# All 32 quads of the recurrent stage written out on four engines, in a graph-RNN and mixture-of-experts kernel

## The chip, the cores and the metric

The kernel runs on one core of one Trainium2 chip. Five engines with instruction streams of their own work in it: TensorE (PE in the rows; its weight loads are PEld), VectorE (DVE), ScalarE (ACT), GpSimd (POOL) and SyncE (SP). They agree by semaphores. The metric is device time in microseconds (us). Before the change the median of three runs is 710.54 us.

## The reference

x is 128 batches of 128 tokens of 128 features, adj is 128 matrices of 128 x 128.

```python
beta = _layernorm(x) @ e_weight / max(sum(adj, 2), EPS)
agg = einsum('blu,blm->bmu', beta, adj)
h_t = tanh(agg[:, t] @ Wx + h_{t-1} @ Wh + b)         # 128 steps, one after the other
x1 = x + h
z = _layernorm(x1)
topk_vals, topk_idx = top_k(z @ gate_w + gate_b, 2)   # 16 experts, 2 for each token
moe = sum_k softmax(topk_vals)_k * expert_{topk_idx_k}(z)
out = x1 + _layernorm(z + moe) * gamma + beta_ffn
```

## The kernel before

The work has three stages. In the first (0 to about 77 us) the batches are normalised and aggregated. In the second, the recurrent stage (about 77 to 285 us), the 128 steps of the recurrence run, and each finished token is normalised, gated, counted and sent as a row to the memory region of its expert. In the third the experts run over the sorted rows. Everything in the front of the kernel belongs to one block; the third stage is a second block, and the engines meet between the two (line 858).

The recurrent stage goes by quads: four steps of the recurrence make a quad, so there are 32. Slots in SBUF are reused every 8 quads (SLOTS).

- PE, `steps(q, u)`: four times a matmul with Wh (L455) onto the aggregate that `fresh` (L446) put in PSUM; between them the transposes of the last quad's states (`turn_h`, L408), the counting matmuls of quad q - 3 (`count`, L437 to L440, which wait for DVE's `hot`), the gate's logits of q - 2 (`logits`, L425) and the transposes of x1 (`turn_x`, L416).
- ACT, `steps(q, u)`: four tanh (L554), and between them copies, exponentials, and for each quad one part of centring W2.
- DVE, `turn(q, u)`: 23 small parts for quads q - 1, q - 2 and q - 3, in an order written out by hand. It opens with `tile_a` (L624: x1 = x + h, which waits for PE's transposes, for the load of x2r, and from the ninth quad for the sends out of its slot), has `gate_3` (L710) and `gate_5` (L730, `hot`) in it, and `place_3` (L766) puts the destination rows of quad q - 3.
- POOL, `turn(q, u)`: `send(q - 3)`, four indirect DMAs (L222) that scatter the rows of one quad each 128 rows at a time; it waits for `tokens` of ACT, `soft_3` and `place_3` of DVE.
- SP loads x2r four quads ahead (L256).

The order of instructions on an engine is the order in the source. `quads(eng, body, 8)` writes quads 0 to 7 out and then runs a loop of three turns whose body holds eight quads. In the loop the quad number is a register, so each wait whose value depends on it needs register arithmetic ahead of it. PE's stage has quads 0 to 7 written out, a loop of two turns of eight (quads 8 to 23), and quads 24 to 31 written out. After its loop DVE has three written-out turns (32 to 34), and POOL three sends. `hold` waits on `s_const` first and then on the semaphore, with a constant or a register alike.

Once DVE's last `place_3` is done, POOL has the last sends to do, DVE makes the tables of the third stage (L820 to L856, with PE's L491), and SP and ACT issue the padding (L211). Then the block ends.

Of the kernel before, what the change touches and what calls it, by code (L numbers as in the profile page):

```python
# [15 lines left out]
NQ = P // QUAD  # L16
SLOTS = 8
# [16 lines left out]

def build(nc, x, adj, eW, Wx, Wh, b, gate_w, gate_b, w1, b1, w2, b2, gamma, beta, out):
    NE, _, F = w1.shape
    NBLK = P + NE
    NQUAD = NBLK // QUAD
# [8 lines left out]
    with ExitStack() as ctx:  # L47
# [177 lines left out]
        def beyond(q, n):  # L225

            return not (isinstance(q, int) and q < n)

        def quads(eng, body, n=UN):

            for u in range(n):
                body(u, u)
            with eng.Fori(1, NQ // n) as J:
                for u in range(n):
                    body(n * J + u, u)
# [54 lines left out]
        def _(pool):  # L290
# [37 lines left out]
            def send(q, u):  # L328

                hold(pool, s_tok, q + 1)  # L330
                pool.wait_ge(s_w1, q + 1)
                hold(pool, s_d, q + 1)
                for j in range(QUAD):
                    scatter(dram_a.ap(), st[:, u, j, C_POS1:C_POS1 + 1].bitcast(I32), st[:, u, j, :],
                            ROWS).then_inc(s_sct[u], 16)
# [39 lines left out]
            def turn(q, u):  # L375
                if beyond(q, 3):
                    send(q - 3, (u - 3) % SLOTS)
            quads(pool, turn, SLOTS)
            for k in range(3):
                send(NQ - 3 + k, SLOTS - 3 + k)  # L380

# [2 lines left out]
        def _(pe):  # L384
# [19 lines left out]
            def turn_h(q, u):  # L404
                if beyond(q, 1):
                    pe.wait_ge(s_x1, q)
                for j in range(QUAD):
                    i = nc.tensor.transpose(ps_ht[:, j * P:(j + 1) * P], HT[:, u % 2, j * P:(j + 1) * P], ident[:, :])  # L408
                i.then_inc(s_ht, 1)

            def turn_x(q, u):
                pe.wait_ge(s_x1, q + 1)
                if beyond(q, 1):
                    pe.wait_ge(s_xe, q)
                for j in range(QUAD):
                    i = nc.tensor.transpose(ps_xt[:, j * P:(j + 1) * P], st[:, u % SLOTS, j, 0:P],  # L416
                                            ident[:, :])
                i.then_inc(s_xt, 1)

            def logits(q, u):  # L420
                pe.wait_ge(s_xe, q + 1)
                if beyond(q, 1):
                    pe.wait_ge(s_l1, q)
                for j in range(QUAD):
                    i = mm(ps_lg[:, j * NE:(j + 1) * NE], x1T[:, u % 2, j * P:(j + 1) * P], gwc[:, :],  # L425
                           start=True, stop=True)
                i.then_inc(s_lg, 1)

            def count(q, u):

                pe.wait_ge(s_hot, q + 1)
                if beyond(q, 2):
                    pe.wait_ge(s_pos, q - 1)

                o, w = ps_agg[u % 2], 2 * NE
                m = hot[:, u % 2, w:]
                mm(o[:, 0:5 * w], ones[:, :], hot[:, u % 2, :], start=True, stop=False, skip_group_check=True)  # L437
                mm(o[:, 0:4 * w], tri[:, :], m, start=False, stop=False, skip_group_check=True)
                for k in range(3, 0, -1):
                    i = mm(o[:, (5 - k) * w:5 * w], ones[:, :], m[:, 0:k * w], start=False, stop=k == 1,  # L440
                           skip_group_check=True)
                i.then_inc(s_cnt, 1)

            def fresh(q, u):

                return mm(ps_rnn[u % 2][:, :], Ec[:, :], AX[:, bass.ds(QUAD * q, QUAD), :], start=True, stop=True,  # L446
                          skip_group_check=True)

            def steps(q, u):

                for k in range(QUAD):
                    if k or beyond(q, 1):
                        pe.wait_ge(s_th, QUAD * q + k)
                        h = (u if k else u - 1) % 2
                        mm(ps_rnn[u % 2][:, k * P:(k + 1) * P], Wh_sb[:, :],  # L455
                           HT[:, h, ((k - 1) % QUAD) * P:((k - 1) % QUAD + 1) * P], start=False, stop=True,
                           skip_group_check=True).then_inc(s_rn, 1)
                    if k == 0 and not (isinstance(q, int) and q == NQ - 1):
                        fresh(q + 1, u + 1)
                    if k == 1 and beyond(q, 1):  # L460
                        turn_h(q - 1, u - 1)
                    if k == 2 and beyond(q, 3):
                        count(q - 3, u - 3)
                    if k == 2 and beyond(q, 2):
                        logits(q - 2, u - 2)
                    if k == 3 and beyond(q, 1):
                        turn_x(q - 1, u - 1)
# [1 line left out]
            quads(pe, agg, SLOTS)  # L469
            pe.wait_ge(s_ae, NQ)  # L470
            fresh(0, 0).then_inc(s_rn, 1)
            for u in range(SLOTS):
                steps(u, u)
            with pe.Fori(1, NQ // SLOTS - 1) as J:
                for u in range(SLOTS):
                    steps(SLOTS * J + u, u)
            for u in range(SLOTS):
                steps(NQ - SLOTS + u, u)
            pe.wait_ge(s_th, P)
            turn_h(NQ - 1, UN - 1)  # L480
            count(NQ - 3, UN - 3)
# [14 lines left out]
        def _(act):  # L496
# [18 lines left out]
            def agg_out(q, u):  # L515
                act.wait_ge(s_m1, q + 1)
                nc.scalar.copy(AX[:, :, bass.ds(QUAD * q, QUAD)],
                               ps_agg[u % 2][:, :].rearrange("p (b t) -> p t b", b=QUAD)).then_inc(s_ae, 1)
# [12 lines left out]
            def exps(q, u):  # L531
                act.wait_ge(s_dd, q + 1)
                if beyond(q, 2):
                    act.wait_ge(s_w1, q - 1)
                a(ex[:, u % 2, :], dd[:, u % 2, :], ACT.Exp).then_inc(s_ex, 1)
# [46 lines left out]

            quads(act, first, SLOTS)
            agg_out(NQ - 1, UN - 1)
            quads(act, steps, SLOTS)
            exps(NQ - 3, UN - 3)
            sums(NQ - 3, UN - 3)
            x1T_out(NQ - 2, UN - 2)
# [10 lines left out]
        def _(dve):  # L599
# [201 lines left out]
            def turn(q, u):  # L801


                order = ((tile_a, 1), (soft_2, 3), (tile_b, 1), (soft_3, 3), (place_1, 3), (tile_b2, 1), (place_2, 3),
                         (tile_b3, 1), (gate_1, 2), (root_0, 1), (place_3, 3), (sq_0, 1), (gate_2, 2),
                         (ag_0, 1), (gate_3, 2), (in_0, 1), (gate_4, 2), (ou_0, 1), (sq_1, 1), (gate_5, 2), (ag_1, 1),
                         (in_1, 1), (ou_1, 1))
                for part, lag in order:
                    if beyond(q, lag) and not (isinstance(q, int) and q - lag >= NQ):
                        part(q - lag, (u - lag) % SLOTS)  # L810
            quads(dve, turn, SLOTS)
            for q in range(NQ, NQ + 3):
                turn(q, q % SLOTS)

            dve.wait_ge(s_d, NQ)
# [398 lines left out]
```

## Time and profile before

| | |
|---|---|
| median of 3 runs | 710.54 us (709.33 to 710.82) |
| the profiled execution | 710.99 us |
| its span in the trace | 709.0 us |
| mean granted TensorE clock | 0.89 of 2.4 GHz |
| busy: PE, DVE, ACT, POOL | 77%, 76%, 58%, 66% of the span |

The profiled execution is 2.0 us longer than its span and 0.45 us longer than the median. Times in the rows are us from the start of the span. A bracket at a row's end is the idle time of the engine ahead of the instruction, and what ended it ("issue": nothing that the profile shows).

### The profile page before, as it was taken

Reading aid. Unit: us, or ns where it says so; the run is one execution under the profiler, and the core shown is the slowest. Engines: PE = TensorE matmul, PEld = TensorE weight load, DVE = VectorE, ACT = ScalarE, POOL = GpSimd, SP = SyncE. Lnnn points to the kernel's source line nnn. Section 1 sums busy time; section 2 is a strip of 40 time slices with the busy share of each in tenths; the row PEclk is TensorE's granted clock in tenths of the full one; section 3 lists DMA queues with packets and bytes.
Section 4 is the critical chain, followed back from the end, with each engine's and each line's share of the span. In section 5 each row is a group of like instructions: output and inputs, shape, how many; then the busy total and the mean of one; then the engine's idle time right before and its main releaser. Section 6 shows DMA issues by size and latency. Waiting matters only on the chain.

```text
span 709.0 us, 18043 instructions
## 1 busy us (share of the span) xinstructions
PE 544.5 (77%) x4140; PEld 486.8 (69%) x4140; DVE 539.0 (76%) x2791; ACT 407.8 (58%) x1345; POOL 466.6 (66%) x526
## 2 busy tenths in 40 slices
PE   1766789887888873399999999800799999999920
PEld 1655566665666652399999999800789999999920
DVE  5988599897997997288888888700299999999950
ACT  2889655454554540266666666500588888888810
POOL 3666647675765767067777777776067777777774
PEclk9989999897987985599999999955799999999975
DMA  8999649432332313379885665430997676664110
GB/s 216 282 281 282 158 147 278 143 104 75 96 94 84 97 49 114 80 210 334 258 251 192 202 190 185 150 149 28 294 328 231 191 215 202 208 203 142 49 49 7
DMA packets 115098, 121.40 MB, mean 171 GB/s; under 512 B 19017, under 2 KB 99613, under 8 KB 115008
## 3 DMA queue, kind: packets, MB, share of 16 engines
q1 hardware_dynamic: 95936, 76.79, 38.7%
q0 software_dynamic: 17920, 43.03, 16.7%
q8 instruction: 34, 0.56, 0.4%
q10 hardware_dynamic: 1152, 0.56, 0.3%
q14 instruction: 56, 0.46, 0.2%
HBM read 68.67 MB, written 55.90 MB: 176 GB/s over the span
## 4 chain that ended last, share of the span: by engine, by line
PE 38%; POOL 7%; ACT 7%; issue 4%; DMA 1%; DVE 1%; SPq 1%; POOLq 0%; ACTq 0%; DVEq 0%
PE bank L987 19%; PE bank L1003 15%; ACT hs L1055 4%; POOL rows_by_second L222 4%; POOL out_dram L222 3%; PE bank L976 3%; ACT xT L1036 2%; PE bank L1000 2%; DMA R<-rows_by_second 0%; DMA rows_by_second<-R 0%; DMA R<-rows_by_first 0%; ACT wr L1044 0%; SPq L912 0%; ACT L1064 0%; SPq L914 0%
## 5 line engine op out<-in xcount | busy, mean ns | idle before, releaser
L222 POOL DMA_INDIRECT rows_by_second<-R x144 | 146.2, 1015 | 62.2 <-issue 36.6
L222 POOL DMA_INDIRECT out_dram<-R x144 | 143.2, 994 | 66.7 <-issue 38.7
L1055 ACT ACTIVATE hs<-bank,wr 128x128 f32<-128x128 f32 x432 | 127.5, 368 | 86.7 <-PE bank L987 82.7
L1003 PE MATMUL bank<-W,hs 128*128 x1152 | 176.1, 289 | 0.0
L222 POOL DMA_INDIRECT rows_by_first<-st x128 | 125.3, 979 | 76.6 <-ACT st L546 40.2
L987 PE MATMUL bank<-xT,wr 128*128 128x128 f32 x1152 | 159.1, 282 | 7.2 <-ACT xT L1036 6.7
L1003 PEld LDWEIGHTS bank<-W,hs 128*128 128x128 f32 x1152 | 151.7, 192 | 3.5
L987 PEld LDWEIGHTS bank<-xT,wr 128*128 128x128 f32 x1152 | 143.1, 196 | 14.6 <-ACT xT L1036 13.4
L1124 DVE SCALAR_TENSOR_TENSOR R<-bank,R 128x128 f32<-128x128 f32 x288 | 87.6, 346 | 66.6 <-PE bank L1003 63.2
L1044 ACT COPY wr<-W1b 128x258 f32 x288 | 105.0, 427 | 14.7 <-PEq L858 14.7
L554 ACT ACTIVATE HT<-bank,bcol 128x128 f32<-128x128 f32 x128 | 46.7, 365 | 69.6 <-PE bank L455 65.7
L976 PE MATMUL bank<-ident,R 128*128 128x128 f32 x288 | 45.0, 281 | 54.0 <-DMA R<-rows_by_second 40.9
L976 PEld LDWEIGHTS bank<-ident,R 128*128 128x128 f32 x288 | 35.1, 146 | 54.7 <-DMA R<-rows_by_second 41.1
L1036 ACT COPY xT<-bank 128x512 f32<-128x512 f32 x72 | 42.9, 595 | 47.7 <-PE bank L976 47.7
L455 PEld LDWEIGHTS bank<-HT,Wh_sb 128*128 128x128 f32 x254 | 45.8, 212 | 35.0 <-ACT HT L554 29.7
L455 PE MATMUL bank<-HT,Wh_sb 128*128 128x128 f32 x254 | 62.3, 331 | 3.3 <-ACT HT L554 2.3
L1000 PE MATMUL bank<-b2s,sel 128*128 128x128 bf16 x288 | 63.2, 219 | 0.4 <-ACT hs L1055 0.3
L400 PE MATMUL bank<-aq,xs 128*128 128x128 f32 x256 | 42.2, 319 | 24.9 <-ACT xs L511 24.8
L400 PEld LDWEIGHTS bank<-aq,xs 128*128 128x128 f32 x256 | 36.4, 221 | 30.7 <-ACT xs L511 19.2
L1113 DVE TENSOR_SCALAR hs<-bank,wr 128x128 f32<-128x128 f32 x144 | 43.8, 346 | 10.3 <-PE bank L987 10.3
L1102 DVE TENSOR_SCALAR R<-R 128x128 f32<-128x128 f32 x144 | 42.2, 366 | 11.7 <-DMA R<-rows_by_first 11.7
L511 ACT ACTIVATE xs<-xq,scq 128x128 f32<-128x128 f32 x128 | 40.8, 391 | 10.0 <-POOL scq L325 9.1
(137 smaller groups left out, 875.4 us busy)
## 6 DMA issues: line engine op xcount, KB each, us to landing
R<-rows_by_second SPq DMA_DIRECT2D x144, 196.0 KB
R<-rows_by_first SPq DMA_DIRECT2D x144, 68.0 KB
xq<-in_x_dram SPq DMA_DIRECT2D x32, 256.0 KB, 4.0
aq<-in_adj_dram SPq DMA_DIRECT2D x32, 256.0 KB, 5.0
x2r<-in_x_dram SPq DMA_DIRECT2D x32, 256.0 KB, 2.9
rows_by_second<-filler SPq DMA_DIRECT2D x1, 3136.0 KB, 13.7
rows_by_second<-filler SPq DMA_DIRECT2D x16, 196.0 KB
rows_by_second<-R POOLq DMA_INDIRECT x144
```

What stands on the lines that cost most here:

```text
L222: return nc.gpsimd.indirect_dma_start(dst, bass.IndirectOffsetOnAxis(ap=idx, axis=0), src, None, bounds_check=limit[n], oob_is_err=False)
L400: i = mm(ps_agg[u % 2][:, j * P:(j + 1) * P], xs[:, u % 2, j * P:(j + 1) * P], aq[:, u, j * P:(j + 1) * P], start=True, stop=True)
L455: mm(ps_rnn[u % 2][:, k * P:(k + 1) * P], Wh_sb[:, :], HT[:, h, ((k - 1) % QUAD) * P:((k - 1) % QUAD + 1) * P], start=False, stop=True, sk ...
L554: a(HT[:, u % 2, k * P:(k + 1) * P], ps_rnn[u % 2][:, k * P:(k + 1) * P], ACT.Tanh, bias=bcol[:, :]).then_inc(s_th, 1)
L976: i = nc.tensor.transpose(ps_z[:, j * P:(j + 1) * P], R[:, u, j, C_Z:C_Y], ident[:, :])
L987: i = mm(ps_h[c][h][:, (j % 2) * P:(j % 2 + 1) * P], wr[:, u % 2, j, c * P:(c + 1) * P], xT[:, u % 2, j * P:(j + 1) * P], start=True, stop ...
L1000: mm(o, sel[:, bass.ds(e[k], 1), :].rearrange("p o m -> p (o m)"), b2s[:, :], start=True, stop=False, skip_group_check=True)
L1003: i = mm(o, hs[:, h, c, k * P:(k + 1) * P], W2[:, bass.ds(e[k], 1), c, :].rearrange("p o f -> p (o f)"), start=False, stop=c == 1, skip_gr ...
L1036: nc.scalar.copy(xT[:, u % 2, :], ps_z[:, :]).then_inc(e_xe, 1)
L1044: i = nc.scalar.copy(wr[:, u % 2, j, :], W1b[:, bass.ds(e, 1), :].rearrange("p o f -> p (o f)"))
L1055: i = a(hs[:, h, c, k * P:(k + 1) * P], ps_h[c][h][:, k * P:(k + 1) * P], ACT.Relu, bias=wr[:, u % 2, 2 * h + k, F + c:F + c + 1])
L1124: i = v.scalar_tensor_tensor(out=y, in0=ps_o[h][:, k * P:(k + 1) * P], scalar=R[:, u, j, w:w + 1], in1=y if r else R[:, u, j, C_Z:C_Y], op ...
```

## The change

On POOL, PE, ACT and DVE the loops of the recurrent stage are replaced by Python loops over all quads, so that every quad has its own instructions and every wait a constant. The work, its order on each engine and all buffers stay. SP's loop stays, and so do the loops of the first stage (`quads(pe, agg)`, `quads(act, first)`, `quads(dve, stats)`, `quads(pool, scale)`) and those of the third.

```diff
@@ gpsimd
-            quads(pool, turn, SLOTS)
+            for q in range(NQ):
+                turn(q, q % SLOTS)
@@ tensor
             fresh(0, 0).then_inc(s_rn, 1)
-            for u in range(SLOTS):
-                steps(u, u)
-            with pe.Fori(1, NQ // SLOTS - 1) as J:
-                for u in range(SLOTS):
-                    steps(SLOTS * J + u, u)
-            for u in range(SLOTS):
-                steps(NQ - SLOTS + u, u)
+            for q in range(NQ):
+                steps(q, q % SLOTS)
@@ scalar
-            quads(act, steps, SLOTS)
+            for q in range(NQ):
+                steps(q, q % SLOTS)
@@ vector
-            quads(dve, turn, SLOTS)
-            for q in range(NQ, NQ + 3):
+            for q in range(NQ + 3):
                 turn(q, q % SLOTS)
```

## Rows read from the trace of the kernel before

**Rows 1.** Waits by engine and line, longest in total first, 76.7 to 288.7 us

```profile
engine line waited for: us in total, times, longest us
ACT HT L554 <- PE bank L455: 65.7, 84, 3.7
...
PE bank L437 <- DVE hot L730: 24.3, 22, 2.9
...
DVE st L624 <- issue: 7.8, 8, 3.3
```

**Rows 2.** Busy time of each engine per stretch: written-out turns 4 to 6, then loop turns

```profile
core 0: us, PE busy (x) PEld busy (x) DVE busy (x) ACT busy (x) POOL busy (x), PEclk, DMA share, GB/s
98.70:104.27 5.57, 4.58 (x36) 3.44 (x33) 5.23 (x42) 3.08 (x12) 4.21 (x5) 1.00 0.73 235
104.27:109.56 5.29, 5.27 (x27) 3.99 (x27) 5.09 (x42) 2.55 (x10) 3.94 (x5) 0.69 1.06 354
109.56:114.84 5.28, 4.97 (x39) 3.77 (x37) 5.08 (x42) 3.42 (x13) 3.93 (x5) 0.98 1.04 337
...
150.76:156.42 5.66, 4.37 (x32) 3.23 (x32) 5.34 (x40) 2.88 (x11) 3.89 (x5) 1.00 0.31 97
156.42:162.04 5.62, 5.62 (x32) 4.28 (x31) 5.35 (x40) 2.59 (x11) 3.88 (x5) 0.70 0.34 99
162.04:171.26 9.22, 5.82 (x44) 4.48 (x41) 5.41 (x40) 4.23 (x16) 6.17 (x7) 1.00 0.26 76
```

**Rows 3.** Timeline of DVE: openings of turns 3, 9, 10 and 15; start, duration

```profile
93.47 0.69 DVE L624 TENSOR_TENSOR st<-bank,x2r 128x512 f32<-128x512 f32 x1
...
128.33 0.69 DVE L624 TENSOR_TENSOR st<-bank,x2r 128x512 f32<-128x512 f32 x1 [2.13 <-DMA x2r<-in_x_dram]
...
133.90 0.69 DVE L624 TENSOR_TENSOR st<-bank,x2r 128x512 f32<-128x512 f32 x1
...
162.04 0.69 DVE L624 TENSOR_TENSOR st<-bank,x2r 128x512 f32<-128x512 f32 x1
```

**Rows 4.** Timeline of DVE at the first jump back of its loop

```profile
167.79 0.17 DVE L680 SCALAR_TENSOR_TENSOR st<-root_a,root_y 128x4 f32<-128x4 f32 x1
171.26 0.69 DVE L624 TENSOR_TENSOR st<-bank,x2r 128x512 f32<-128x512 f32 x1 [3.31 <-issue]
```

**Rows 5.** Timeline of DVE: the second jump back, then turns 31 and 32

```profile
210.65 0.69 DVE L624 TENSOR_TENSOR st<-bank,x2r 128x512 f32<-128x512 f32 x1
...
219.80 0.69 DVE L624 TENSOR_TENSOR st<-bank,x2r 128x512 f32<-128x512 f32 x1 [3.23 <-issue]
...
261.88 0.27 DVE L766 TENSOR_REDUCE st<-picked 128x8 int32<-128x128 f32 x1
...
265.15 0.69 DVE L624 TENSOR_TENSOR st<-bank,x2r 128x512 f32<-128x512 f32 x1
```

**Rows 6.** DMA queues, 167 to 171.5 us: queue, kind, packets, MB, share

```profile
q14 instruction: 3, 0.02, 2.1%
```

**Rows 7.** DMA queues, 133.9 to 156.42 us, the same columns

```profile
q14 instruction: 3, 0.02, 0.3%
```

**Rows 8.** Timeline of all engines where PE's and ACT's loops jump back

```profile
163.78 0.30 PEld L455 LDWEIGHTS bank<-HT,Wh_sb 128*128 128x128 f32 x2 [0.26 <-ACT HT L554]
...
164.31 0.37 ACT L554 ACTIVATE HT<-bank,bcol 128x128 f32<-128x128 f32 x1 [0.29 <-PE bank L455]
```

**Rows 9.** Timeline of PE's transposes of the states, just ahead of turn 15

```profile
160.75 0.70 PE L408 MATMUL bank<-ident,HT 128*128 128x128 f32 x4
```

**Rows 10.** Timeline of DVE's place_3 in turn 9, and POOL's sends behind it

```profile
131.05 0.28 DVE L766 TENSOR_REDUCE st<-picked 128x8 int32<-128x128 f32 x1
...
132.14 0.97 POOL L222 DMA_INDIRECT rows_by_first<-st  x1 [2.88 <-ACT st L546]
133.42 0.97 POOL L222 DMA_INDIRECT rows_by_first<-st  x1 [0.30 <-issue]
```

**Rows 11.** Timeline of POOL: the last four quads, first three sends and last send

```profile
263.06 0.97 POOL L222 DMA_INDIRECT rows_by_first<-st  x1 [0.74 <-issue]
265.71 0.98 POOL L222 DMA_INDIRECT rows_by_first<-st  x1 [1.68 <-issue]
267.00 0.97 POOL L222 DMA_INDIRECT rows_by_first<-st  x1 [0.30 <-DVE st L742]
...
283.59 0.97 POOL L222 DMA_INDIRECT rows_by_first<-st  x1 [0.30 <-issue]
```

**Rows 12.** Timeline of DVE, ACT and SP at the end of the stage

```profile
282.69 0.30 DVE L856 TENSOR_SCALAR sti<-si 1x296 int32<-1x296 int32 x1
...
288.67 1.33 ACT L1044 COPY wr<-W1b 128x258 f32 x4 [14.68 <-PEq L858]
...
288.96 3.28 SPq L912 DMA_DIRECT2D R<-rows_by_first  x6
```

## The prediction

> **What bounds the kernel now.** I read the waits first, because the edit touches four engines and only the one that the others wait for can matter. In the recurrent stage ACT waits for PE (65.7 us, every tanh for its matmul), and PE waits for DVE's `hot` (24.3 us), which stands ahead of the counting matmuls in PE's order [rows 1]. DVE's own largest wait has no releaser: 7.8 us of "issue" ahead of `tile_a`, the first instruction of a turn [rows 1]. So the question is what DVE is doing. The busy time by stretch, each stretch one turn of DVE (from one L624 to the next), answers it: DVE is busy 5.08 to 5.41 us in every turn, whether the turn takes 5.28 or 9.22, while PE, in the shorter turns at a granted clock of 0.98 or more, has 4.4 to 5.0 [rows 2]. DVE is the bound; it sets the pace of `hot`, so of PE's count, so of the recurrence.
>
> Then I compare turns that are written out with turns in the loop, since both kinds are in this trace with the same work. Turns 3 to 6, written out, run from 93.47 [rows 3] to 114.84 [rows 2]: 21.37 / 4 = 5.34 us each. Turns 10 to 14, in the loop, run from 133.90 to 162.04 [rows 3]: 28.14 / 5 = 5.63 us each. Turn 15 of DVE ends with the jump back, and takes 9.22 us [rows 2]; all of its excess, 9.22 - 5.63 = 3.59 us, lies in one gap of 3.31 us (and the register work that belongs to every turn) between L680, the last instruction of the body, and L624, the first [rows 4]. The second jump makes a turn of 219.80 - 210.65 = 9.15 us, an excess of 3.52 us [rows 5].
>
> What is in that gap? The DMA queues show three instruction packets of queue 14 in the 4.5 us around the jump, where 22.5 us inside the loop have three as well [rows 6, 7]: code is fetched again when the jump is taken. The Trainium skill (Runtime: NRT & Kernel Launch, section Instruction fetch mechanics) says that a taken branch to code outside the two blocks held forces a fetch before execution goes on, while the next block of straight code is fetched ahead. The trace agrees with the first half by the 3.31 us gap.
>
> The end of the stage is not DVE's but POOL's. DVE finishes the tables at 282.69 + 0.30 = 282.99; POOL's last send starts at 283.59 and takes 0.97, so it ends at 284.56 [rows 11, 12]. The third stage opens at 288.67 (ACT) and 288.96 (SP's loads) [rows 12], some 4.1 us after POOL.
>
> **The change part by part.**
>
> DVE's jumps (removed): 3.59 + 3.52 = 7.11 us of DVE's path, nothing beside them.
>
> DVE's register work (removed in turns 8 to 31): a loop turn costs 5.63 - 5.34 = 0.29 us more than a written-out one. Its own spread bounds this: the written-out turns themselves are 5.57, 5.29 and 5.28 [rows 2]. With all new turns at 5.28 the difference is 0.35, with all at 5.57 it is 0.06. I take the mean over four turns, as it has both kinds in it.
>
> What is late next on DVE: `tile_a` of turn 9 waits 2.13 us for the load of x2r [rows 3]. SP's order is not touched, so that load lands when it did, and all that turns 1 to 8 save is lost there. I count from 128.33 on. Turn 32 opens at 265.15 [rows 5]: 23 turns in 136.82 us. Written out: 23 x 5.34 = 122.8. DVE gains 14.0 us, of which 7.1 are the jumps and 6.9 the registers.
>
> POOL: its sends of quad 6 start at 132.14, 0.81 us after `place_3` of turn 9 ends at 131.05 + 0.28 [rows 10]. `place_3` of turn 31 is at 261.88 [rows 5], 22 turns and 130.83 us later; written out these are 22 x 5.34 = 117.5, a gain of 13.35 us. POOL could become the bound instead: a send comes every 133.42 - 132.14 = 1.28 us, so a quad takes 5.11 us at least [rows 10]. That is under 5.34, so it keeps up, by 0.23 us a turn. From 263.06 POOL has 16 sends, and needs 284.56 - 263.06 = 21.50 us; at 1.277 each less the last pause of 0.30 they are 20.13. The other 1.37 us is one pause of 1.68 us in the last turn of its loop, ahead of 265.71, which no other send of the stage has and which nothing releases [rows 11]. It stands where the body of the loop runs for the last time. If it belongs to the loop it goes, if to the sends it stays: POOL gains 14.7 or 13.35. I take that it goes, since within the written-out sends nothing like it is seen, and keep the other for the range. DVE's last work, 14.0 us earlier at 269.0, stays ahead of POOL's end at 284.56 - 14.7 = 269.9, so POOL ends the stage still.
>
> PE and ACT: their jumps cost nothing now. Where PE's loop jumps back it waits 0.26 us for the tanh, as it does in other quads, and ACT at its own jump 0.29 us for PE [rows 8]. Their register work lies in the time in which PE waits for DVE. Both edits at nothing; what hides them is DVE's pace, and that cover gets thinner. PE at a mean granted clock of 0.70 is busy for all 5.62 us of a turn, and its transposes end at 160.75 + 0.70 = 161.45, 0.59 us before DVE needs them at 162.04 [rows 2, 3, 9]. A turn that is 0.29 shorter leaves 0.30. Against a loss stands the written-out turn of 104.27 to 109.56: at 0.69 it took 5.29 all the same [rows 2]. I put 0.5 us on it in all (an estimate), between 0 and 2.2 (one of the three loop turns shown is such a one; eight of 24 at 5.62 - 5.34 each).
>
> Fetching more code: DVE's code gets longer, but it executed each of these instructions before; in turns 3 to 6 it ran straight code at 5.34 with the fetches in it. Nothing.
>
> The waits for a slot's sends, which quads 8 and later have and quads 0 to 7 have not, come as constants. They are met eight quads before, so only the issue of the instruction that carries them could cost; turn 4, the slowest of the written-out ones, has 5.57 without them, so a cost of up to 0.23 us a turn can't be told from such scatter. I take 0, and leave the other end to rival A.
>
> The third stage starts earlier and is else the same, with its clock in the same low state at its start. So I move the end by POOL's gain.
>
> Sum, against the profiled execution: 710.99 - 14.7 + 0.5 = 696.8 us. That execution is 0.45 us above the median of the runs, so the median after should be 696.3 us.
>
> **The rivals.**
>
> A, only the jumps go. The 0.29 us of a loop turn is not register arithmetic but something that late quads carry in any form (the slots' waits, or how DVE's code falls), as the 5.57 turn, written out, hints. Then the gain is 7.1 us: 710.5 - 7.1 = 703.4. Against it: turns 12 and 13 took 5.66 and 5.62 beside 97 and 99 GB/s of DMA, and turns 5 and 6, written out, 5.29 and 5.28 beside 354 and 337 [rows 2].
>
> B, PE takes the bound in its slow stretches. At half clock (1.2 GHz granted, which is what a mean of 0.70 is made of together with 2.4) PE fills a turn of 5.62. If each such turn stays at 5.62 the price is 2.2 us, 1.7 more than in the sum, and with POOL's pause kept another 1.4: 696.3 + 1.7 + 1.4 = 699.4.
>
> C, slower. Straight code stalls DVE at each new block of code as the jump does. Rows 7 put an instruction packet on queue 14 every 7.5 us or less often; even if only every second one is DVE's, 136 us have 9. At 3.3 us each that is 30 us, less the 14 gained: 726. It decides from 14 / 9 = 1.6 us a block. Against it: the written-out turns 3 to 6, 21 us, took at most 5.57 each, so none has such a gap in it [rows 2]. The skill's rule of the same section (straight code is fetched ahead, a crossing is mostly hidden) would make this case nothing; only the rows bear on the chance.
>
> D, the change doesn't do what it says: the tool that builds the kernel could keep the loop or its register waits. The written-out quads 0 to 7 show that it doesn't.
>
> E, better: all turns at 5.28. Then DVE gains 136.82 - 121.4 = 15.4, POOL 130.83 - 116.2 + 1.37 = 16.0: 694.5.
>
> **How the numbers follow.** Forecast, 695.5 to 698.5: 0.58. B, with partial forms, 698.5 to 702: 0.17. A, 702 to 705: 0.10. E, below 695.5: 0.10. C: 0.03. D: 0.02. The likeliest time is 696.3. The range takes in E down to 693.8 and B up to 702.0, and leaves A, C and D out, 0.15, and a little below. Faster by over 0.2% (which is about what a measurement of this kernel can tell from no change): 0.95. Same: 0.02. Slower: 0.03.
>
> **What would show it.** In the profile after: no "issue" gap over 1 us ahead of L624; DVE's turns from 128.33 on at 5.3 to 5.4 us, turn 32 near 251.2; the wait for x2r in turn 9 still there and somewhat longer; PE and ACT with fewer register instructions and the same waits on DVE; POOL's last send ending near 270 without a pause of 1.7; the third stage as long as before. The prediction is wrong if turns stay at 5.6 (A), if `tile_a` begins to wait for L408 (B), or if gaps of some 3 us come at even distances on DVE (C).

## The result, and the profile after

| | before | after |
|---|---|---|
| median of 5 runs | 710.54 us | 697.5 us (696.34 to 698.12) |
| the profiled execution | 710.99 us | 697.93 us |
| its span | 709.0 us | 696.1 us |
| busy: PE, DVE, ACT, POOL | 77, 76, 58, 66% | 77, 77, 59, 67% |

The ratio is 0.982, with a 95% interval of 0.981 to 0.983: the kernel is 13.0 us faster. The forecast was 696.3, in a range of 693.8 to 702.0.

The waits, sorted as in [rows 1], come first again (columns: us in total, times, longest):

```profile
engine line waited for: us in total, times, longest us
ACT HT L550 <- PE bank L456: 55.4, 76, 3.2
...
PE bank L438 <- DVE hot L727: 21.2, 27, 2.8
...
DVE st L621 <- DMA x2r<-in_x_dram: 2.7, 1, 2.7
```

`tile_a` is L621 now. Its 7.8 us of "issue" are gone, and what is left ahead of it is the wait for x2r. ACT still waits for PE and PE for DVE's `hot`, so DVE is still what the others follow.

DVE's turns by stretch, the columns of [rows 2]:

```profile
138.02:143.33 5.31, 4.53 (x35) 3.39 (x33) 5.10 (x42) 3.02 (x12) 3.96 (x5) 1.00 0.34 105
143.33:148.81 5.48, 4.53 (x35) 3.38 (x33) 5.21 (x42) 3.02 (x12) 3.89 (x5) 1.00 0.34 102
148.81:154.11 5.30, 5.30 (x28) 3.90 (x27) 5.09 (x42) 2.42 (x10) 3.96 (x5) 0.68 0.35 102
170.01:175.53 5.52, 4.53 (x35) 3.38 (x33) 5.19 (x42) 3.02 (x12) 3.96 (x5) 1.00 0.33 100
```

Two kinds of turn are to be seen. Most take 5.30, also the one in which the granted TensorE clock is 0.68 on the mean and PE is busy for all of it (148.81 to 154.11): DVE does not wait for PE. Six of the 23 from turn 9 on take 5.44 to 5.77.

The timeline of DVE shows the wait in turn 9 and the openings of turns 10 and 32, which answer to [rows 3 and 5]:

```profile
127.19 0.69 DVE L621 TENSOR_TENSOR st<-bank,x2r 128x512 f32<-128x512 f32 x1 [2.67 <-DMA x2r<-in_x_dram]
...
132.72 0.69 DVE L621 TENSOR_TENSOR st<-bank,x2r 128x512 f32<-128x512 f32 x1
...
250.77 0.69 DVE L621 TENSOR_TENSOR st<-bank,x2r 128x512 f32<-128x512 f32 x1
```

From turn 9 to turn 32 it is 250.77 - 127.19 = 123.58 us for 23 turns, 5.37 each, against 136.82 before. POOL and the opening of the third stage, which answer to [rows 11, 12]:

```profile
249.11 0.97 POOL L222 DMA_INDIRECT rows_by_first<-st  x1 [0.64 <-issue]
251.76 0.98 POOL L222 DMA_INDIRECT rows_by_first<-st  x1 [1.68 <-issue]
...
269.70 0.97 POOL L222 DMA_INDIRECT rows_by_first<-st  x1 [0.31 <-issue]
```

```profile
274.77 1.33 ACT L1040 COPY wr<-W1b 128x258 f32 x4 [14.91 <-PEq L854]
```

POOL's pause of 1.68 us stands where it stood, ahead of the 114th send. The stage ends with POOL at 269.70 + 0.97 = 270.67, 13.9 us earlier than before, and the third stage opens 288.67 - 274.77 = 13.9 us earlier. The span gains 12.9: the third stage took 421.3 us where it took 420.3. That is scatter: with the same code it took between 418.2 (e2) and 421.3 in the traces of the first sessions.

### The profile page after: what moved, and what is told of

Same layout as the page of the kernel before. It is cut to its first block, busy times and chain, and to the rows that moved or that the text cites. A ratio compares the mean times of both kernels' runs of the same rounds, so it can differ in the third digit from the quotient of the medians.

```text
span 696.1 us, 17518 instructions
## 1 busy us (share of the span) xinstructions
PE 537.3 (77%) x4140; PEld 480.1 (69%) x4140; DVE 533.6 (77%) x2791; ACT 407.7 (59%) x1345; POOL 468.3 (67%) x526
## 4 chain that ended last, share of the span: by engine, by line
PE 38%; POOL 8%; ACT 7%; issue 4%; DMA 1%; DVE 1%; SPq 1%; POOLq 0%; ACTq 0%; DVEq 0%
PE bank L983 19%; PE bank L999 15%; ACT hs L1051 4%; POOL rows_by_second L222 4%; POOL out_dram L222 4%; PE bank L972 3%; ACT xT L1032 2%; PE bank L996 2%; DMA R<-rows_by_second 1%; DMA rows_by_second<-R 0%; DMA R<-rows_by_first 0%; SPq L908 0%; ACT L1060 0%; SPq L910 0%; POOLq L884 0%
## 5 line engine op out<-in xcount | busy, mean ns | idle before, releaser
L456 PEld LDWEIGHTS bank<-HT,Wh_sb 128*128 128x128 f32 x254 | 43.3, 202 | 34.4 <-ACT HT L550 30.2
L456 PE MATMUL bank<-HT,Wh_sb 128*128 128x128 f32 x254 | 60.6, 322 | 3.4 <-ACT HT L550 2.3
```

Source lines behind the costliest of these rows:

```text
L456: mm(ps_rnn[u % 2][:, k * P:(k + 1) * P], Wh_sb[:, :], HT[:, h, ((k - 1) % QUAD) * P:((k - 1) % QUAD + 1) * P], start=False, stop=True, sk ...
```

## The experiments

Each is measured against the kernel before on the same chip in the same session. For e1, e2, e3 and e7 that kernel had 708.99 us, so the changed kernel's 0.982 stands there for 696.2. e4, e5, e6 and e9 are single executions, beside one of the kernel before at 709.05.

**Which engine's loop was it?** First DVE's loop alone is written out, then the other three alone.

```diff
@@ e1: the kernel before, vector
-            quads(dve, turn, SLOTS)
-            for q in range(NQ, NQ + 3):
+            for q in range(NQ + 3):
                 turn(q, q % SLOTS)
@@ e2: the changed kernel, vector
-            for q in range(NQ + 3):
+            quads(dve, turn, SLOTS)
+            for q in range(NQ, NQ + 3):
                 turn(q, q % SLOTS)
```

> Only DVE's loop is written out; POOL, PE and ACT keep theirs. If DVE alone set the pace, this is the whole change: 697.5 us (696.5 to 698.5), DVE's turns from the ninth on at 5.3 to 5.4 us. If the register work of PE, ACT or POOL had come to carry part of the bound once DVE got faster, it stays above: 699 or more.

> POOL, PE and ACT are written out, DVE keeps its loop with its two jumps back and its register work. If DVE alone sets the pace: 710.5 us, no change, with the two gaps of 3.3 us still there. If the others' loops cost something of their own: some us faster.

e2 took 709.39 us, ratio 1.000 (0.998 to 1.001): without DVE's part the change is nothing. Its timeline of DVE has both gaps still:

```profile
170.44 0.69 DVE L621 TENSOR_TENSOR st<-bank,x2r 128x512 f32<-128x512 f32 x1 [3.37 <-issue]
...
219.20 0.69 DVE L621 TENSOR_TENSOR st<-bank,x2r 128x512 f32<-128x512 f32 x1 [3.46 <-issue]
```

e1 took 699.09 us, 0.986 (0.983 to 0.989): most of the gain, some 3 us short of the whole, and above the 696.5 to 698.5 that I had expected. But in the recurrent stage nothing is short. DVE's 22 turns from turn 10 take 118.24 us in it:

```profile
134.79 0.69 DVE L624 TENSOR_TENSOR st<-bank,x2r 128x512 f32<-128x512 f32 x1
...
253.03 0.69 DVE L624 TENSOR_TENSOR st<-bank,x2r 128x512 f32<-128x512 f32 x1
```

In the changed kernel they take 250.77 - 132.72 = 118.05. The profiled e1 came into the stage late, from code that both have alike: its first `tile_a` stands at 85.76 and turn 9 opens at 129.25, 2.06 us behind the changed kernel. A second comparison stands below.

**Jumps or register work?** The changed kernel, with DVE's turns 8 to 31 written out as they are, but with the quad's number in a register that holds what is read from memory, so that every wait has its arithmetic back and there is no jump.

```diff
-            for q in range(NQ + 3):
+            for q in range(SLOTS):
+                turn(q, q)
+            J = dve.value_load(zero_i[0:1, 0:1], min_val=0, max_val=3)   # holds 0
+            for q in range(SLOTS, NQ):
+                turn(SLOTS * J + q, q % SLOTS)
+            for q in range(NQ, NQ + 3):
                 turn(q, q % SLOTS)
```

> The changed kernel, but DVE's turns 8 to 31, written out, take the quad's number from a register that is read from memory (it holds 0), so each wait on it has its register arithmetic ahead of it as in the loop, without any jump. If the arithmetic costs what the loop turns showed (0.29 us a turn, 24 turns): 697.5 + 7.0 = 704.5 us. If it costs nothing and all the gain was in the jumps and in where DVE's code falls: 697.5 to 698.5 us.

It took 702.05 us, 0.990 (0.987 to 0.992), 5.9 us above the changed kernel, where 7.0 were expected. Its turns 10 and 32 open here (`tile_a` is L625 in it):

```profile
132.00 0.69 DVE L625 TENSOR_TENSOR st<-bank,x2r 128x512 f32<-128x512 f32 x1
...
255.94 0.69 DVE L625 TENSOR_TENSOR st<-bank,x2r 128x512 f32<-128x512 f32 x1
```

That is 123.94 / 22 = 5.63 us a turn, what loop turns took before, against 118.05 / 22 = 5.37. So the arithmetic costs 0.27 us a turn, 6.4 us over 24 turns; rival A, under which the late turns would have stayed slow without it, is out. From turn 9 to turn 32, as the prediction counts, it is 136.82 us before, 255.94 - 126.32 = 129.62 in e3, and 123.58 in the changed kernel: 7.2 us for the jumps and 6.0 for the arithmetic (with the few instructions of code that it adds).

**Does the next cover matter?** SP loads x2r for quads 8 to 11 ahead of the weights of the third stage.

```diff
             filled(dram_b.ap()[TAIL:ROWS, :], W_B, NE).then_inc(s_fill, 16)
+            for u in range(UN):
+                tiles(2 * UN + u, u)
             sp.dma_start(W1b[:, :, 0:F], w1.rearrange("e h f -> h e f")).then_inc(r_w, 16)
...
-            with sp.Fori(2, NQ // UN) as J:
+            with sp.Fori(3, NQ // UN) as J:
```

> The changed kernel, with SP's loads of x2r for quads 8 to 11 issued ahead of the loads of W1, b1, gamma and beta instead of behind them. DVE's wait of 2.67 us in turn 9 for x2r should go. If DVE sets the pace and POOL follows: 697.5 - 2.7 = 694.8 us. If POOL's sends come to bound the stage, less: with POOL at 5.11 us a quad it keeps up, so any loss would show as POOL busy without a pause. If the late W1 loads matter to the third stage: slower.

It took 693.75 us, 0.977 (0.975 to 0.980): 3.4 us less than the changed kernel by the ratios, 2.7 expected. The two intervals don't overlap. Turn 9 opens without a wait, one turn of 5.30 after turn 8's opening at 119.78:

```profile
125.08 0.69 DVE L623 TENSOR_TENSOR st<-bank,x2r 128x512 f32<-128x512 f32 x1
```

This is the fastest version measured here, and what turns 1 to 8 save is lost in that wait as long as it is there. The traces show less than 3.4 us in the stage: turn 32 opens at 248.82, 1.95 us before the changed kernel's, and the third stage opens at 272.80, 1.97 before. The other 1.1 us of the profiled span lies in the third stage (420.2 against 421.3), whose scatter is as large.

**What does a jump pay for?** Four loops of two turns each are put ahead of DVE's recurrent stage, with bodies of 60, 200, 300 and 600 memsets. The kernel takes 768.35 us by it; only the gaps count.

```diff
+            for t, n_body in enumerate((60, 200, 300, 600)):
+                with dve.Fori(0, 2) as J:
+                    for k in range(n_body):
+                        i = v.memset(body[:, k:k + 1], 0.0)
+                    i.then_inc(s_body, 1)
+                    dve.wait_ge(s_body, J + 2 * t + 1)
```

> The changed kernel with four loops of two turns ahead of DVE's recurrent stage, whose bodies are 60, 200, 300 and 600 one-column memsets: one jump back each, to code that lies that many instructions behind. The kernel gets far longer by it; only the gap at each jump counts. If the jump's 3.3 us is a fetch of code that was dropped: no gap of that size at 60, one of about 3 us at 600, and the change from one to the other somewhere between. If any taken jump costs it: about 3 us at all four. If it was DVE's waits at the turn's opening: none at any.

The timeline of DVE, from the second turn of the loop of 60 to the second of the loop of 600 (start, duration, memsets merged, idle time ahead):

```profile
70.55 1.85 DVE L782 MEMSET body<- 128x1 bf16 x60 [0.57 <-DVE body L782]
...
79.83 5.77 DVE L782 MEMSET body<- 128x1 bf16 x200 [0.56 <-DVE body L782]
85.98 0.29 DVE L782 MEMSET body<- 128x1 bf16 x9 [0.39 <-DVE body L782]
86.62 3.64 DVE L782 MEMSET body<- 128x1 bf16 x128 [0.35 <-issue]
90.58 3.63 DVE L782 MEMSET body<- 128x1 bf16 x128 [0.32 <-issue]
94.53 1.01 DVE L782 MEMSET body<- 128x1 bf16 x35 [0.32 <-issue]
98.71 0.29 DVE L782 MEMSET body<- 128x1 bf16 x9 [3.16 <-issue]
100.97 3.63 DVE L782 MEMSET body<- 128x1 bf16 x128 [1.98 <-issue]
...
132.56 2.51 DVE L782 MEMSET body<- 128x1 bf16 x88 [3.93 <-issue]
```

The jump to a body of 60 or 200 memsets leaves a gap of 0.57 and 0.56 us, of which 0.39 is there without a jump as well (85.98: the wait for the memset before). The jump over 300 leaves 3.16 us, and 1.98 more nine memsets on; that over 600 leaves 3.93. So a taken jump as such costs 0.2 us, and one back over 300 or 600 instructions costs 3.5 to 4.5 us more than straight code does. The change lies between 200 and 300. A turn of DVE in the kernel before has 40 instructions that the profile counts [rows 2], so its loop's body has 320 and more.

The rows show a second thing: in straight code there is an idle time of 0.32 us after every 128 memsets. The second turn of the body of 200 has none in it: 5.77 us for 200 memsets, where 128 take 3.63. These are the instruction packets of queue 14 from 113 to 129 us, straight code, and from 94.5 to 98.71, the gap at the jump over 300:

```profile
q14 instruction: 4, 0.03, 0.7%
...
q14 instruction: 2, 0.02, 1.2%
```

One packet comes for each 128 memsets of straight code, and two in the 3.16 us gap. Between 79.83 and 85.6, the second turn of the body of 200, the queues show none. So the pauses go with code that has to be fetched, and a body of 200 is not fetched again.

The same in the stage itself, with eight short loops:

```diff
             for q in range(NQ + 3):
+                if 10 <= q < 26 and q % 2 == 0:
+                    with dve.Fori(0, 2) as _:
+                        dve.wait_ge(s_w, 16 * 6)
                 turn(q, q % SLOTS)
```

> The changed kernel with a loop of two turns around one wait that is long met, ahead of eight of DVE's turns (10, 12, ... 24), so eight jumps back of one or two instructions in the stage itself. If only a jump to dropped code costs: at most 0.4 us each, 697.5 to 700.5 us. If any jump costs 3 us: 720 us or more.

It took 701.47 us. `tile_a` behind such a loop is late by 0.48 us:

```profile
143.30 0.69 DVE L621 TENSOR_TENSOR st<-bank,x2r 128x512 f32<-128x512 f32 x1 [0.49 <-issue]
...
148.75 0.69 DVE L621 TENSOR_TENSOR st<-bank,x2r 128x512 f32<-128x512 f32 x1
```

From turn 9 to 32 it takes 129.18 us, 5.6 more than the changed kernel: 0.7 for each loop, its setting up included. That is more than the 0.4 I had put as the most, and a fifth of 3.3.

**Where do the slow turns of the written-out code come from?** 96 memsets more on DVE, in its wait for W2 ahead of the stage.

```diff
             dve.wait_ge(s_w, 16 * 6)
+            for k in range(96):
+                v.memset(pads_96[:, k:k + 1], 0.0)
             dve.wait_ge(r_b2, 16 * 4)
```

> The changed kernel with 96 small memsets more on DVE where it waits for the load of W2, before the recurrent stage. In the changed kernel the written-out turns take 5.30 us but for turns 4, 10, 13, 18, 23 and 31, which have 0.2 to 0.3 us in one place. If that is the crossing from one block of code to the next (every 4 to 5 turns, some 256 instructions), these places move to earlier turns, by 96 instructions or not quite two turns. If it is something in the work or the clock, they stay in the same turns. The time: 697.5 us in both cases, within 1.5.

It took 695.85 us. The slow places moved, but not as a block (but for its "turn 4", the expectation names a slow turn by the opening that comes late behind it): turn 9 went from 5.53 to 5.30, turn 10 from 5.30 to 5.84:

```profile
132.35 0.69 DVE L622 TENSOR_TENSOR st<-bank,x2r 128x512 f32<-128x512 f32 x1
...
138.19 0.69 DVE L622 TENSOR_TENSOR st<-bank,x2r 128x512 f32<-128x512 f32 x1
...
143.50 0.69 DVE L622 TENSOR_TENSOR st<-bank,x2r 128x512 f32<-128x512 f32 x1
```

Others went: of turns 9 to 31 four are over 5.40 where six were. Where DVE's code is the same, in e1, e6, e7 and the changed kernel, the same turns are slow to 0.05 us (9, 12, 17, 22, 23 and 30), though the four come into the stage at 83.25 to 85.76. So the slow turns go with where the code falls, not with the work or the time. The reading that fits with e9 is that each 128 instructions bring a short pause, which shows where it meets short instructions and is hidden under long ones. That it is hidden in this way is argued, not shown.

**POOL's pause.** In the two runs below eight more sends come ahead of the stage's first. Those of e6 are skipped row by row, as their indices lie past the end. Those of e10 write to a scratch tensor.

```diff
@@ e6
+            for _ in range(8):
+                scatter(dram_a.ap(), filler[:, C_TOKEN:C_TOKEN + 1].bitcast(I32), filler[:, 0:W_A],
+                        ROWS).then_inc(s_null, 16)
+            pool.wait_ge(s_null, 128)
@@ e10
+            for k in range(8):
+                scatter(null_rows.ap(), tok[:, k:k + 1], filler[:, 0:W_A], P * P).then_inc(s_null, 16)
+            pool.wait_ge(s_null, 128)
```

> The changed kernel with eight more indirect DMAs on POOL before its first send, whose rows go nowhere (their indices lie past the end). In both kernels the one pause of 1.68 us stands between sends 113 and 114 of the stage. If it belongs to the number of DMAs that POOL has issued: it moves to between sends 105 and 106, two quads earlier. If it belongs to POOL's code or to the time: it stays at 113 and 114, or goes. Time 697 to 698.5 us.

> The changed kernel with eight more indirect DMAs on POOL before its first send, which this time do write (their own rows of a scratch tensor), unlike those of e6, whose rows were skipped. With e6 the pause stayed ahead of the stage's 114th send. If the pause comes from the number of rows that POOL has written descriptors for, it moves to the 106th send of the stage, two quads earlier. If it stays at the 114th, it belongs to that send.

In both the pause stays: it is POOL's 122nd DMA now, which is the stage's 114th again. Here it is in e10:

```profile
301.74 0.97 POOL L224 DMA_INDIRECT rows_by_first<-st  x1 [2.13 <-DVE st L768]
304.38 0.97 POOL L224 DMA_INDIRECT rows_by_first<-st  x1 [1.67 <-issue]
```

e6 took 698.86 us. e10's 903.39 belongs to the later session below. In e1, where POOL keeps its loop, it is the same send. So neither the number of DMAs, nor the rows written, nor the loop makes the pause; it goes with that one send. What in it does, stays open.

**A second comparison of e1, and the first stage written out too.** These two, with the changed kernel as the measure and with e10 beside them, ran in a later session, in which the kernels took 27 to 29% longer: the kernel before had 904.19 us there.

> The changed kernel itself, once more, as the measure for the next run on the same chip: 0.982 of the kernel before, 697 us.

> Only DVE written out, once more, beside the changed kernel. Its first look gave 0.986 of before against 0.982, while DVE's 22 turns from turn 10 took 118.24 us against 118.05 in the changed kernel. If DVE alone is the change, the two lie within 1 us of each other. If the loops of the other three cost 2 us somewhere, e12 stays 2 us above.

```diff
@@ e13: e7, and on pool, tensor, scalar and vector alike
-            quads(dve, stats, SLOTS)
+            for q in range(NQ):
+                stats(q, q % SLOTS)
```

> x2r ahead of W1 as in e7, and the first stage's loops written out as well on POOL, PE, ACT and DVE. The first stage waits for its loads (DMA at 1.0 of its engines from 20 to 76 us), so its loops should cost nothing: as e7, 0.977 of the kernel before, 694 us. If its jumps stall DVE or ACT where the loads have no slack: some us less. A time above e7's would mean that more code costs.

The changed kernel took 896.44 us, 0.991 (0.989 to 0.993): only 8 us of gain. e12 took 899.67, 0.995 (0.992 to 0.998), and e13 897.61, 0.991 (0.988 to 0.993). The timeline of the changed kernel as it ran there shows why they lie so near to each other:

```profile
202.91 0.37 ACT L550 ACTIVATE HT<-bank,bcol 128x128 f32<-128x128 f32 x1 [3.43 <-remote]
...
203.33 0.49 PE L456 MATMUL bank<-HT,Wh_sb 128*128 128x128 f32 x2 [2.68 <-ACT HT L550]
```

```profile
249.06 0.69 DVE L621 TENSOR_TENSOR st<-bank,x2r 128x512 f32<-128x512 f32 x1 [1.09 <-PE bank L409]
...
256.14 0.69 DVE L621 TENSOR_TENSOR st<-bank,x2r 128x512 f32<-128x512 f32 x1 [1.16 <-PE bank L409]
```

The second pair of rows is one turn of 256.14 - 249.06 = 7.08 us; from turn 9 to turn 32 the mean is (297.09 - 136.59) / 23 = 6.98, where it was 5.37. DVE waits for PE's transposes at many openings. Four of its turns, in the columns of [rows 2]:

```profile
198.78:205.90 7.12, 4.44 (x32) 3.71 (x30) 5.25 (x42) 3.01 (x11) 4.02 (x5) 0.91 0.26 77
205.90:214.14 8.24, 7.78 (x33) 6.28 (x33) 5.25 (x41) 3.01 (x11) 4.96 (x6) 0.50 0.25 77
249.06:256.14 7.08, 5.83 (x33) 4.54 (x33) 5.25 (x40) 2.97 (x11) 3.96 (x5) 0.76 0.28 82
263.06:269.06 6.00, 4.66 (x38) 3.67 (x38) 5.19 (x40) 3.16 (x13) 3.14 (x4) 1.00 0.31 94
```

DVE is busy for 5.19 to 5.25 us in each, hardly more than before. In the last three rows PE is busy for 4.66 us at a granted clock of 1.00 and for 7.78 at 0.50 (the lower of its two levels), and the turn grows with it. Over the whole stage the mean granted clock is 0.76 (84.3 to 324.4 us), where it was 0.87 in the trace of the first session (83.25 to 274.77). This is the mechanism of rival B, PE taking the bound at the lower clock, and it came there. Seven times PE also stands for 2.6 to 2.8 us, as at 203.33, with ACT waiting 3.35 to 3.53 us (the turn of the first row); from 200.70 to 203.30 it has no instruction at a clock of 1.00. What holds it there this trace doesn't name, and no run shows why the clock was lower. DVE is not the bound there, so a faster DVE gains less, and the earlier x2r of e13 nothing that shows. Nor does e13 tell what the first stage's loops cost by themselves. The e11 and e13 expectations were written for the first sessions' level and missed for that reason.

e1 lay about 3 us above the changed kernel in both sessions (e12: 3.2, where 1 or 2 were expected), with intervals that overlap by a little in both. No profiled pair has these 3 us in the recurrent stage. That of e12 opens the third stage at 323.70, before the 324.39 of the changed kernel, and then takes 575.7 us for it where that took 570.8, with the same code. Whether the loops of PE, ACT and POOL cost something is open; e2 shows that they cost nothing as long as DVE has its own.

## Why the prediction held, step by step

**DVE is the bound, and PE and ACT at nothing**: right for the session of the result. e2 is the direct evidence (1.000), though e1 leaves up to 3 us open. Three turns at a mean clock of 0.68 or 0.69 took 5.30 to 5.32 us, so rival B did not come there; PE's slow stretches cost less than the 0.5 us that I put there. The margin was thin: PE was busy for 5.28 to 5.30 us of these turns. In the later session B's mechanism did come.

**The jumps, 7.1 us**: right in size (7.2 by e3) and cause. Both gaps are gone in the changed kernel and there in e2. e9 shows that it is the distance that costs, not the jump, and that instruction packets come in the gap. The Trainium skill (Runtime: NRT & Kernel Launch, section Instruction fetch mechanics) says that a taken branch to code outside the window that is held forces a fetch before execution goes on. The traces agree: 0.57 us at a body of 60 against 3.16 at 300.

**The register work, 6.9 us**: right in kind, a little high in size; e3 has it at 0.27 us a turn and 6.0 us over the 23 turns. The written-out turn was put at 5.34 and came to 5.37, as the mean of 5.30 and the slow ones. So DVE's gain from turn 9 on was 13.2 us and not 14.0. The choice of the mean over the best turn (rival E) was the better one.

**x2r takes what turns 1 to 8 save**: right, and the wait grew from 2.13 to 2.67 us as said. I did not price its removal. e7 shows that it was worth 3.4 us by the ratios, 2.0 by the opening of the third stage.

**POOL's pause goes**: wrong, and the one step whose cause failed. I had argued from its place, the last turn of POOL's loop. It stands at the same send with and without a loop (e1, the changed kernel, e6, e10). The term was 1.37 us, by itself more than the miss of 1.2 us.

**POOL keeps up at 5.11 us a quad**: right. Up to its 113th send it goes on waiting ahead of each quad's sends, and ends the stage still, at 270.67 against DVE's tables at 269.1.

**More code costs nothing**: right in the sum; rival C is out. No gap near 3 us came in some 24 turns of straight code. The slow turns, which I read as such crossings, are 0.14 to 0.47 us above 5.30. Between turn 9 and turn 32 queue 14 has 13 instruction packets, where the kernel before had 18.

**The third stage as it was**: yes within its scatter; it took 1.0 us longer in the profiled execution, and the first stage 0.9 us less, with the same code in both.

In the sum: POOL's end moved by 13.9 us, where 14.7 less 0.5 was said. Counted from turn 9, as the prediction counts, it moved by 12.75 (156.23 us before, 143.48 after); the pause is 1.37 of what is missing. The other 1.14 us are turn 9's own, which opened at 127.19 and not at 128.33. In e2, whose DVE code is that of before, it opened at 127.50, so this is scatter of the load and not the change. It happened to make up for the 1.0 us of the third stage. That the forecast came within 1.2 us is in part this luck; the gain on DVE and its two parts are not.

## What to carry to other kernels

Compare written-out turns with loop turns in one trace before writing a loop out: here the two kinds gave 5.34 and 5.63 us, and with the two gaps at the jumps the gain on DVE could be read from them. Write out the loop of the engine that sets the pace; on engines that wait, even three loops at once gave nothing here. And look at once for the first wait that the time saved runs into: moving one group of loads (e7) gave 2.0 us in the trace and 3.4 by the ratios. Then look how much room the next engine has: PE was busy for all of a turn at the lower clock, and in a session with more of that clock half of the gain was gone.

## What the runs showed of the hardware that I had not expected

- On DVE a jump back over up to 200 instructions cost 0.2 us beside the wait that was there anyway, and one over 300 left gaps of 3.16 us and then 1.98 (e9).
- Straight code on DVE pauses for 0.32 us after each 128 instructions when these are as short as 28 ns, with one instruction packet for each 128 (e9). Six turns of 5.44 to 5.77 us among those of 5.30 are read as the same pause, which is not shown.
- Register arithmetic ahead of waits, 0.27 us a turn (e3), is visible on an engine that is busy for 5.1 of 5.3 us.
- One and the same program took 697.5 us in one session and 896.4 in another, and the change was worth 1.8% in the one and 0.9% in the other, because PE, at a mean granted clock of 0.76 in the recurrent stage and not 0.87, had become the bound in many turns.
